# A new plan of a batch, and maxima taken from three PSUM banks at once, in a kernel of cross attention and experts

## The chip, the cores and the metric

The kernel runs on one core of a Trainium2 chip. The metric is the device time of one execution in microseconds (us); three runs of a kernel give a median. The engines of a core are TensorE (PE in the profile, its weight loads PEld), VectorE (DVE), ScalarE (ACT), GpSimd (POOL) and SyncE (SP), which here issues the DMA transfers. PSUM, into which TensorE writes, has 8 banks of 512 float32 columns.

## The reference, cut to what matters

```
x = x + tanh(g_xattn) * xattn(layernorm(x), ctx)     # x: 16 x 100 x 128, ctx: 16 x 1444 x 96, 16 heads of 64
x = x + tanh(g_ffn)   * ffn(layernorm(x))

xattn: q = x w_q; k = ctx w_k; v = ctx w_v           # per head
       softmax(q k^T / 8) v, then w_o and b_o
ffn:   rmsnorm, self attention over 100 tokens (16 heads of 8), wo, residual,
       rmsnorm, router (softmax, top 2 of 8 experts), experts of width 256 and one shared
```

The softmax of the cross attention is computed with a maximum subtracted for each row of `q`, the 1600 rows of a batch being 16 heads times 100 tokens.

## The kernel before, in words

The 16 batches run one after the other. The weights are folded in advance, so that a batch needs `qk = x M` (1600 rows of 96 numbers) and scores `qk ctx^T` against the 1444 context rows. All large products are in float16 with a second float16 part for the remainder (`_hi`, `_lo`), so a product takes three matmuls.

**Units.** A batch has 24 units `i` (two halves of the rows times 12 chunks of 128 context rows). In unit `i` TensorE computes the scores of chunk `i` (`score_unit`, L736 to L738, six matmuls), ScalarE takes their exponential twice (`probs`: `p32` in float32, `p_hi` in float16), VectorE or GpSimd the remainder `p_lo` (L430; GpSimd in the units of `LO_POOL`), and TensorE multiplies the probabilities of unit `i - 2` by the context (`pv_unit`, L755: `p_hi` with `c_hi`, `p_hi` with `c_lo`, `p_lo` with `c_hi`). Scores use banks 0 to 2, two for a unit, so the second half of the scores of unit `i` waits until ScalarE is through with unit `i - 1`. Banks 3 and 4 hold the sums.

**The ring of three.** All other small work of a batch is cut into numbered pieces, which a table `plan` places in the units: `q` (the rows `qk` of the next batch), `p` (maxima), `m` (the transpose of the maxima), `y0` and `y1` (the output projection of one half), `f0` to `f16` (the self attention of the batch before), `ln`, `rs`, `xf`, `h2` (norms). The pieces of a unit are divided into thirds: some stand behind the scores, some behind the first third of the value matmuls (`middle`), some behind the last. The same list is walked by TensorE, ScalarE and VectorE. Each piece with a matmul takes the next of the banks 5 to 7 in turn, and TensorE waits only until the piece three places back has been read:

```
ring, bank = (2, 1 + k % 2) if kind in ("prep", "end") else (3, (base[0] + k) % 3)
last = order[k - ring] if k >= ring else None
```

**The maxima.** The rows of the next batch form 13 tiles (`RT`) of 128, and the 1444 columns three parts (`MP`) of 512, 512 and 420. Piece `p` n is one matmul into one bank (L835) and one VectorE reduction to `mx` (L1281); after the last, VectorE reduces `mx` to `mx_row` and negates it to `mneg`. `m` transposes `mneg` (L839), VectorE copies it to `mrow` (L1291), and SP sends it as an extra row into `qk_hi` (`send_row`), where the first scores of the next batch wait for it (`row_in`). Ahead of the first batch a form `w` does the same with the other banks, two sets of three in turn: three matmuls (L815) and one reduction over 1444 columns (L1256).

**The context.** `ctx_hi_parts` (ScalarE) and `ctx_lo` (GpSimd) convert the context of batch `b + 1` at the start of batch `b`; SP then has it transposed into `cT_both` (L491), for which the first `p` of the batch waits (`ct_in`), and copied to `c_both`. One planner's rule places the `p`: each goes to the unit of 4 to 20 with the least `load`, a sum of estimated costs.

GpSimd also normalises the sums of a half (`normalise`) and does `norm_1` and `norm_2` for the self attention. The first batch and the last have lists of their own; the experts follow the last batch.

Of the kernel before, what the change touches and what calls it, by code (L numbers as in the profile page):

```python
# [29 lines left out]
def flamingo_kernel(nc, x, ctx, g_xattn, g_ffn, w_q, w_k, w_v, w_o, b_o, norm1_w, norm2_w,  # L30
# [35 lines left out]
    for n, i in enumerate((0, 0, 1, 1)):  # L66
        plan[i].append(("q", n))
    plan[7].append(("y1", 0))
    plan[20].append(("y0", 0))
    plan[7].append(("ln", 0))  # L70
    plan[7].append(("xf", 0))
    for n, i in enumerate((9, 10, 11, 12, 13, 14, 13, 14, 15, 16, 15, 16, 17, 18, 19, 20, 23)):
        plan[i].append(("f", n))
# [58 lines left out]
    PREPARE = ("y0", "q", "p", "m")  # L132
# [42 lines left out]
    def batch_of(unit, b):  # L175

        return b + {"q": 1, "p": 1, "m": 1, "y0": 0}.get(unit[0], -1)
# [10 lines left out]
                "pad qk_hi0", "pad qk_hi1", "lnr0", "minus one", "pad p_hi", "pad p_lo", "mx", "ones v9", "ones mask",  # L188
# [13 lines left out]
    with ExitStack() as stack:  # L202
# [36 lines left out]
        mx = sb("mx", [P, RT, MP])  # L239
# [100 lines left out]
        def run_aux(aux, units, b, kind, parity):  # L340
# [5 lines left out]
            order = [u for u in at if u[0] not in NO_BANK]  # L346
            for u in units:
# [194 lines left out]
        def _(pool):  # L542
# [31 lines left out]
            step("mx", g.memset(mx[:, :, :], 0.0))  # L574
# [111 lines left out]
        def _(pe):  # L686
# [101 lines left out]
            def aux(seq, free, par, unit, b, parity, out_of, last):  # L788
# [15 lines left out]
                if kind == "w":  # L804
                    if n == 0:
                        pe.wait_ge(ct_in, 16)
                    if n == 1:
# [3 lines left out]
                    if n >= 2:  # L811
# [572 lines left out]
```

## Time and profile before

| | before |
|---|---|
| median of 3 runs | 1397.75 us (1396.24 to 1400.17) |
| the profiled execution, its own time | 1400.51 us |
| its span | 1398.8 us |
| mean granted TensorE clock | 0.982 |
| busy: PE, DVE, ACT, POOL | 90%, 74%, 58%, 47% |
| DMA | 57.27 MB, 41 GB/s on the mean |

The busy share is the union of an engine's instructions over the span. The span goes from the first to the last instruction; what lies around it (1400.51 against 1398.8) isn't in the trace. The granted clock is 1.00 at 2.4 GHz and 0.50 at 1.2 GHz.

### The profile page before, as it was taken

How to read it: one execution, taken by the hardware profiler on the slowest of the kernel's cores; microseconds unless marked ns; L12 is line 12 of the kernel's file. 1: busy time of each engine (PE TensorE's matmuls, PEld its weight loads, DVE VectorE, ACT ScalarE, POOL GpSimd, SP SyncE). 2: the span in 40 equal slices, each digit the busy share in tenths (PEclk: the TensorE clock that was granted, in tenths of full speed). 3: DMA queues.
4: the chain of work that ended last, by engine and by line, in shares of the span. 5: the costliest groups of instructions: out<-in, count | busy, mean ns of one | idle time of the engine just before them, and what ended most of it. 6: DMA issues, size and time to landing. Idle time of an engine off the chain costs nothing.

```text
span 1398.8 us, 34572 instructions
## 1 busy us (share of the span) xinstructions
PE 1265.0 (90%) x14472; PEld 912.5 (65%) x14472; DVE 1034.4 (74%) x1762; ACT 818.2 (58%) x1476; POOL 661.4 (47%) x555
## 2 busy tenths in 40 slices
PE   6789798989999999999998989899999999889998
PEld 4366576766666666667675767676666666557776
DVE  5797777768686868596868687786868685866776
ACT  1346466665666565666565656656665666555664
POOL 3135355454544554444444545445354454544654
PEclk9799999999999999999999999999999999999999
DMA  6204303030313030302112030303031200010000
GB/s 162 62 2 111 78 13 76 13 75 13 76 12 76 12 76 12 71 11 50 35 32 56 13 76 13 76 13 76 13 76 13 60 13 15 1 26 2 8 8 13
DMA packets 122277, 57.27 MB, mean 41 GB/s; under 512 B 108262, under 2 KB 117706, under 8 KB 122122
## 3 DMA queue, kind: packets, MB, share of 16 engines
q1 hardware_dynamic: 122122, 55.07, 17.5%
q8 instruction: 114, 1.87, 0.6%
q14 instruction: 41, 0.34, 0.1%
HBM read 15.38 MB, written 0.82 MB: 12 GB/s over the span
## 4 chain that ended last, share of the span: by engine, by line
PE 59%; DVE 20%; ACT 11%; DMA 5%; issue 4%; POOL 0%; SPq 0%; ACTq 0%; DVEq 0%; POOLq 0%
PE psum L755 13%; DVE p_lo L430 9%; PE psum L736 7%; PE psum L835 7%; PE psum L737 6%; PE psum L738 6%; DMA cT_both<-c_new 5%; PE psum L771 4%; DVE mx L1281 3%; PE psum L867 3%; ACT p_hi L964 3%; PE psum L783 3%; ACT p_hi L959 2%; ACT p L963 2%; PE psum L889 2%
## 5 line engine op out<-in xcount | busy, mean ns | idle before, releaser
L430 POOL TENSOR_TENSOR p_lo<-p,p_hi 128x768 f16<-128x768 f32 (+1 forms) x144 | 273.7, 1905 | 412.8 <-ACT p_hi L959 261.5
L1281 DVE TENSOR_REDUCE mx<-psum 128x1 f32<-128x512 f32 (+1 forms) x585 | 355.0, 651 | 70.6 <-PE psum L835 66.6
L958 ACT ACTIVATE p<-psum 128x768 f32<-128x768 f32 (+1 forms) x256 | 214.0, 836 | 276.7 <-PE psum L738 276.7
L430 DVE TENSOR_TENSOR p_lo<-p,p_hi 128x768 f16<-128x768 f32 (+1 forms) x240 | 326.3, 1359 | 28.6 <-ACT p_hi L959 25.5
L755 PEld LDWEIGHTS psum<-c_both,p_hi 128*128 128x128 f16 x4992 | 283.1, 99 | 88.9 <-issue 31.6
L755 PE MATMUL psum<-c_both,p_hi 128*128 128x97 f16 (+1 forms) x4992 | 326.1, 207 | 5.5 <-ACT acc_sb L974 5.4
L736 PE MATMUL psum<-qk_hi,cT_both 97*128 97x384 f16 (+1 forms) x768 | 259.7, 338 | 30.1 <-ACT p_hi L959 19.4
L737 PE MATMUL psum<-qk_lo,cT_both 96*128 96x384 f16 (+1 forms) x768 | 258.5, 337 | 0.0
L738 PE MATMUL psum<-qk_hi,cT_both 96*128 96x384 f16 (+1 forms) x768 | 256.3, 334 | 0.0
L835 PE MATMUL psum<-cT_both,qk_hi 96*128 96x512 f16 (+1 forms) x585 | 201.9, 371 | 30.7 <-DVE mx L1281 14.3
L963 ACT ACTIVATE p<-psum 128x384 f32<-128x384 f32 (+1 forms) x256 | 130.0, 508 | 151.0 <-PE psum L738 151.0
L959 ACT ACTIVATE p_hi<-psum 128x768 f16<-128x768 f32 (+1 forms) x256 | 213.4, 834 | 0.0
L755 PE MATMUL psum<-c_both,p_lo 128*128 128x97 f16 x2496 | 172.8, 208 | 20.1 <-POOL p_lo L430 16.9
L755 PEld LDWEIGHTS psum<-c_both,p_lo 128*128 128x128 f16 x2496 | 129.9, 99 | 23.1 <-POOL p_lo L430 19.2
L736 PEld LDWEIGHTS psum<-qk_hi,cT_both 97*128 97x128 f16 x768 | 75.6, 98 | 97.5 <-ACT p_hi L959 49.5
L964 ACT ACTIVATE p_hi<-psum 128x384 f16<-128x384 f32 (+1 forms) x256 | 131.0, 512 | 0.0
L738 PEld LDWEIGHTS psum<-qk_hi,cT_both 96*128 96x128 f16 x768 | 76.1, 99 | 57.9 <-issue 2.2
L737 PEld LDWEIGHTS psum<-qk_lo,cT_both 96*128 96x128 f16 x768 | 76.1, 99 | 45.8 <-issue 1.4
L645 POOL TENSOR_TENSOR p_lo<-p,p_hi 128x400 f16<-128x400 f32 x72 | 69.2, 962 | 67.9 <-ACT p_hi L986 67.9
L835 PEld LDWEIGHTS psum<-cT_both,qk_hi 96*128 96x128 f16 x585 | 54.0, 98 | 58.8 <-DVE mx L1281 21.5
L594 POOL TENSOR_TENSOR acc_rc<-acc_sb,minus_one 128x6 f32<-128x6 f32 (+1 forms) x31 | 52.9, 1706 | 50.3 <-ACT acc_sb L974 50.3
L1227 DVE TENSOR_TENSOR qk_lo<-psum,qk_hi 96x400 f16<-96x400 f32 x64 | 34.0, 566 | 49.8 <-ACT qk_hi L935 49.7
(201 smaller groups left out, 2082.2 us busy)
## 6 DMA issues: line engine op xcount, KB each, us to landing
c_both<-c_new SPq DMA_DIRECT2D x16, 768.0 KB, 4.0
ctx_nat<-in_ctx_dram SPq DMA_DIRECT2D x16, 528.0 KB
aT<-a_new SPq DMA_TRANSPOSE x64, 2.9
wg<-in_L_ffn_e_gate_dram SPq DMA_DIRECT2D x1, 1024.0 KB, 5.5
wu<-in_L_ffn_e_up_dram SPq DMA_DIRECT2D x1, 1024.0 KB, 7.9
wd<-in_L_ffn_e_down_dram SPq DMA_DIRECT2D x8, 128.0 KB, 5.1
out_dram<-x SPq DMA_DIRECT2D x4, 200.0 KB
x<-in_x_dram SPq DMA_DIRECT2D x1, 600.0 KB
```

The costliest lines, as they stand in the source:

```text
L430: engine.tensor_tensor(p_lo[0:m, i % 3, 0:w], p32[0:m, i % 3, 0:w], p_hi[0:m, i % 3, 0:w], ALU.subtract).then_inc(lo_made(b, i)[0], 1)
L645: g.tensor_tensor(hid_lo[:, n % HS, :], hidden[:, n % 3, :], hid_hi[:, n % HS, :], ALU.subtract).then_inc(hid_lo_out, 1)
L736: mm(outs[k], cT_hi[parity][:, cols], qk_hi[parity][:, qs[k]], start=True, stop=False)
L737: mm(outs[k], cT_hi[parity][0:C, cols], qk_lo[parity][:, qs[k]], start=False, stop=False)
L738: t = mm(outs[k], cT_lo[parity][:, cols], qk_hi[parity][0:C, qs[k]], start=False, stop=True)
L755: t = mm(psum[:, ACCB + bank, k * (C + 1):k * (C + 1) + wide], p[0:m, i % 3, n * P:(n + 1) * P], c[parity][0:m, j, 0:wide], start=(j == 0 ...
L835: t = mm(bank[:, 0:w], qk_hi[parity][0:C, padded_rows(rt)], cT_hi[parity][0:C, part * MW:part * MW + w], start=True, stop=True)
L958: a(to32, src, ACT.Exp, scale=DH ** -0.5)
L959: ins = a(to_hi, src, ACT.Exp, scale=DH ** -0.5)
L963: a(to32[:, k, :], src, ACT.Exp, scale=DH ** -0.5)
L964: ins = a(to_hi[:, k, :], src, ACT.Exp, scale=DH ** -0.5)
L1281: v.tensor_reduce(mx[:, rt, part:part + 1], bank[:, 0:w], AX.X, ALU.max)\
```

## The change

A planner's rule for 39 single-bank pieces `p` is replaced by 13 pieces `w`, one for each row tile, placed first in the 13 units of 3 to 21 that a sum of costs finds lightest. `w`, which only the start of the kernel used, now also works inside the batches: TensorE waits until all three ring banks are read, fills banks 5, 6 and 7, VectorE reads all three with one reduction straight to `mx_row`, and the next ring piece waits for that reduction (`wide`). `mx` and its final reduction go. The other entries of the plan move too: one `q` in each of units 0 to 3 in place of two in 0 and two in 1; `y1`, `ln`, `xf` and `norm_1` from unit 7 to 6, `f0` and `f1` to 8 and 9, `m` from 21 to 22, GpSimd's remainders from (5, 7, 9, 11, 13, ...) to (4, 5, 8, 10, 12, ...). The context of batch `b + 2` is converted in units 18 (ScalarE) and 19 (GpSimd) of batch `b`, not that of `b + 1` at its start.

```
-    for n, i in enumerate((0, 0, 1, 1)):
+    for n, i in enumerate((0, 1, 2, 3)):
         plan[i].append(("q", n))
...
-    CTX_AT, NORM1_AT, ACC0_AT, NORM2_AT = 0, 7, 14, 22
-    LO_POOL = (5, 7, 9, 11, 13, 16, 18, 20, 22)
+    CTX_HI_AT, CTX_LO_AT, NORM1_AT, ACC0_AT, NORM2_AT = 18, 19, 6, 14, 22
+    LO_POOL = (4, 5, 8, 10, 12, 16, 18, 20, 22)
...
-    plan[21].append(("m", 0))
+    places = range(3, 22)
+    for n, i in enumerate(sorted(sorted(places, key=lambda i: (load[i], i))[0:RT])):
+        plan[i].insert(0, ("w", n))
+    plan[22].append(("m", 0))
...
+                before = ringed[:ringed.index(u)] if u in ringed else []
+                wide = (b + 1) * RT + sum(o[0] == "w" for o in before) if before and before[-1][0] == "w" else 0
...
+        def wide_bank(b, n):
+            return AUXB if b else 3 * (n % 2)
...
                 for i in range(UNITS):
+                    if i == CTX_LO_AT and b + 2 < B:
+                        ctx_lo(b + 2, parity)
...
+                    if b:
+                        pe.wait_ge(aux_free, free)
+                        pe.wait_ge(*last)
+                        pe.wait_ge(wide_free, b * RT + n)
                     for part in range(MP):
                         cols = slice(part * MW, min(KV, (part + 1) * MW))
-                        t = mm(psum[:, 3 * (n % 2) + part, 0:cols.stop - cols.start], qk_hi[parity][0:C, padded_rows(n)],
-                               cT_hi[parity][0:C, cols], start=True, stop=True)
+                        t = mm(psum[:, wide_bank(b, n) + part, 0:cols.stop - cols.start],
+                               qk_hi[parity][0:C, padded_rows(n)], cT_hi[parity][0:C, cols], start=True, stop=True)
                     t.then_inc(wide_full, 1)
                 if kind in NO_BANK:
                     return
                 if seq >= 2:
                     pe.wait_ge(*last)
+                if wide:
+                    pe.wait_ge(wide_free, wide)
...
-                elif kind == "p":
-                    rt, part = divmod(n, MP)
-                    if n == 0:
-                        pe.wait_ge(aux_free, free)
-                        pe.wait_ge(ct_in, (b + 1) * 16)
-                    w = min(MW, KV - part * MW)
-                    t = mm(bank[:, 0:w], qk_hi[parity][0:C, padded_rows(rt)],
-                           cT_hi[parity][0:C, part * MW:part * MW + w], start=True, stop=True)
...
                 for i in range(UNITS):
-                    if i == CTX_AT and kind != "last":
-                        ctx_hi_parts(b + 1, kind, 1 - parity)
+                    if kind == "first" and i == 0:
+                        ctx_hi_parts(1, kind, 1)
+                    if i == CTX_HI_AT and b + 2 < B:
+                        ctx_hi_parts(b + 2, kind, parity)
...
                 if kind == "w":
-                    dve.wait_ge(wide_full, n + 1)
-                    scores_of = psum[:, 3 * (n % 2):3 * (n % 2) + MP, :].rearrange("p b w -> p (b w)")[:, 0:KV]
+                    dve.wait_ge(wide_full, b * RT + n + 1)
+                    scores_of = psum[:, wide_bank(b, n):wide_bank(b, n) + MP, :].rearrange("p b w -> p (b w)")[:, 0:KV]
                     v.tensor_reduce(mx_row[:, n:n + 1], scores_of, AX.X, ALU.max).then_inc(wide_free, 1)
```

In a middle batch `w0` to `w12` stand in units 4, 5, 6, 7, 8, 10, 11, 13, 15, 16, 17, 19 and 21. In 4, 5, 7 and 10 `w` stands alone and so last; in 8 (`w4`, `f0`), 11 (`w6`, `f2`), 17 (`w10`, `f12`), 19 (`w11`, `f14`) and 21 (`w12`, `rs`) it stands in the middle; in 6 (`w2`, `y1`), 13 (`w7`, `f4`, `f6`), 15 (`w8`, `f8`, `f10`) and 16 (`w9`, `f9`, `f11`) it stands first.

The first place is TensorE's stream in unit 13 of a middle batch, from the last score on (`f6` is L885 before, L883 after). Before, `f4` (L880) is the first piece there, and a `p` (L835) the last:

```order
L738 MATMUL psum<-qk_hi,cT_both 128x416
L880 MATMUL psum<-kbd,qT 100x400 [waits aux_free]
L755 MATMUL psum<-c_both,p_hi 128x97 x6
L885 MATMUL psum<-ident,ex 100x100 [waits exp_out,aux_free]
L885 MATMUL psum<-ident,ex 100x100 x3
L755 MATMUL psum<-c_both,p_hi 128x96 x6
L755 MATMUL psum<-c_both,p_lo 128x97 [waits lo_pool]
L755 MATMUL psum<-c_both,p_lo 128x97 x5
L835 MATMUL psum<-cT_both,qk_hi 128x512 [waits aux_free]
```

After (`f4` is L878):

```order
L738 MATMUL psum<-qk_hi,cT_both 128x416
L819 MATMUL psum<-cT_both,qk_hi 128x512 [waits wide_free,aux_free]
L819 MATMUL psum<-cT_both,qk_hi 128x512
L819 MATMUL psum<-cT_both,qk_hi 128x420
L755 MATMUL psum<-c_both,p_hi 128x97 x6
L878 MATMUL psum<-kbd,qT 100x400 [waits wide_free,aux_free]
L755 MATMUL psum<-c_both,p_hi 128x96 x6
L755 MATMUL psum<-c_both,p_lo 128x97 [waits probs_lo]
L755 MATMUL psum<-c_both,p_lo 128x97 x5
L883 MATMUL psum<-ident,ex 100x100 [waits exp_out,aux_free]
```

The three matmuls of a tile stand together at the start of the unit, and `f4` has moved behind them with a wait for their reader; six value matmuls lie between.

The second place is VectorE's stream from the copy for `f0` to the maxima of `f2` (L1306 before, L1296 after), with `kbd`, the block-diagonal keys of `f1`, between. Before:

```order
L1297 COPY hT<-psum 128x100 [waits aux_full]
L430 TENSOR_TENSOR p_lo<-p,p_hi 128x768 [waits pv,probs_hi]
L1281 TENSOR_REDUCE mx<-psum 128x1 [waits aux_full] x2
L1299 COPY qT<-psum 128x100 [waits aux_full]
L1300 COPY v<-psum 100x16x8
L1301 TENSOR_TENSOR kbd<-psum,head_mask 128x1600
L1281 TENSOR_REDUCE mx<-psum 128x1 [waits aux_full]
L430 TENSOR_TENSOR p_lo<-p,p_hi 128x768 [waits pv,probs_hi]
L1306 TENSOR_REDUCE mx<-psum 100x4 [waits aux_full]
```

After:

```order
L1287 COPY hT<-psum 128x100 [waits aux_full]
L1289 COPY qT<-psum 128x100 [waits aux_full]
L1290 COPY v<-psum 100x16x8
L1291 TENSOR_TENSOR kbd<-psum,head_mask 128x1600
L430 TENSOR_TENSOR p_lo<-p,p_hi 128x768 [waits pv,probs_hi]
L1256 TENSOR_REDUCE mx_row<-psum 128x1 [waits wide_full] x2
L1296 TENSOR_REDUCE mx<-psum 100x4 [waits aux_full]
```

Two wide reductions (`w5`, `w6`), with a remainder and `kbd` ahead of them, stand in front of the maxima of `f2` in place of three narrow ones.

The third place is TensorE's stream at the end of a batch, from the value matmuls of unit 22 to the first score of the next batch. Before, the transpose of the maxima (L839) stands in front of unit 22; after (below), it is L837 and stands behind it:

```order
L755 MATMUL psum<-c_both,p_lo 128x97 x6
L837 MATMUL psum<-ident,mneg 13x128 [waits max_step,wide_free,aux_free]
L736 MATMUL psum<-qk_hi,cT_both 128x416 [waits probs_hi]
L737 MATMUL psum<-qk_lo,cT_both 128x416
L738 MATMUL psum<-qk_hi,cT_both 128x416
L736 MATMUL psum<-qk_hi,cT_both 128x416 [waits probs_hi]
L737 MATMUL psum<-qk_lo,cT_both 128x416
L738 MATMUL psum<-qk_hi,cT_both 128x416
```

One unit lies between the transpose and the first score that needs the row, where two lay before.

## Rows read from the trace of the kernel before

**Rows 1.** The page, busy time, share of the span and instructions of each engine

```profile
PE 1265.0 (90%) x14472; PEld 912.5 (65%) x14472; DVE 1034.4 (74%) x1762; ACT 818.2 (58%) x1476; POOL 661.4 (47%) x555
```

**Rows 2.** One middle batch: busy PE, PEld, DVE, ACT, POOL, clock, DMA

```profile
584.00:658.00 74.00, 68.62 (x829) 49.79 (x827) 55.23 (x91) 46.16 (x84) 35.95 (x28) 1.00 0.21 42
```

**Rows 3.** The chain that ended last: start, us, what

```profile
155.71 1.51 PE psum L867 x27
...
606.07 3.90 DVE p_lo L430
...
1191.74 1.52 PE psum L867 x27
```

**Rows 4.** Timeline of TensorE in one batch, its longest waits, in brackets

```profile
586.68 0.68 PE L755 MATMUL psum<-c_both,p_hi 128*128 128x97 f16 x12 [0.38 <-ACT acc_sb L974]
...
590.31 0.34 PE L736 MATMUL psum<-qk_hi,cT_both 97*128 97x384 f16 x1 [0.38 <-ACT p_hi L959]
...
592.05 0.38 PE L835 MATMUL psum<-cT_both,qk_hi 96*128 96x512 f16 x1 [1.08 <-DMA cT_both<-c_new]
...
607.61 0.43 PE L755 MATMUL psum<-c_both,p_lo 128*128 128x97 f16 x6 [1.02 <-POOL p_lo L430]
...
613.41 0.89 PE L880 MATMUL psum<-kbd,qT 128*100 128x400 f32 x2 [1.19 <-DVE kbd L1301]
...
650.86 0.35 PE L736 MATMUL psum<-qk_hi,cT_both 97*128 97x416 f16 x1 [0.40 <-ACT p_hi L964]
```

**Rows 5.** Timeline of TensorE, unit 5 of that batch and the next score

```profile
593.44 0.33 PE L736 MATMUL psum<-qk_hi,cT_both 97*128 97x384 f16 x1
...
594.42 0.38 PE L835 MATMUL psum<-cT_both,qk_hi 96*128 96x512 f16 x1
594.64 0.42 PE L755 MATMUL psum<-c_both,p_hi 128*128 128x97 f16 x6
...
595.64 0.34 PE L835 MATMUL psum<-cT_both,qk_hi 96*128 96x420 f16 x1
595.82 0.33 PE L736 MATMUL psum<-qk_hi,cT_both 97*128 97x384 f16 x1
```

**Rows 6.** Timeline of VectorE in that batch, narrow reductions

```profile
592.46 0.69 DVE L1281 TENSOR_REDUCE mx<-psum 128x1 f32<-128x512 f32 x1 [3.53 <-PE psum L835]
...
596.50 3.48 DVE L1281 TENSOR_REDUCE mx<-psum 128x1 f32<-128x512 f32 x6
```

**Rows 7.** Wide reductions ahead of batch 0: timelines, then the group by form

```profile
26.50 4.80 DVE L1256 TENSOR_REDUCE mx_row<-psum 128x1 f32<-128x1444 f32 x3 [0.65 <-PE psum L815]
...
37.19 11.09 DVE L1256 TENSOR_REDUCE mx_row<-psum 128x1 f32<-128x1444 f32 x7
...
28.22 1.38 PE L815 MATMUL psum<-cT_both,qk_hi 96*128 96x512 f16 x3 [0.56 <-DVE mx_row L1256]
...
L1256 DVE TENSOR_REDUCE mx_row<-psum 128x1 f32<-128x1444 f32 x13 | 20.7, 1655 | 0.8 <-PE psum L815 0.6
```

**Rows 8.** Timelines: the row of maxima, a middle batch, then the first

```profile
573.86 0.22 PE L839 MATMUL psum<-ident,mneg 128*13 128x128 f16 x1
...
578.83 0.33 PE L736 MATMUL psum<-qk_hi,cT_both 97*128 97x384 f16 x1
...
49.01 0.21 DVE L1291 COPY mrow<-psum 13x128 f16<-13x128 f16 x1 [0.45 <-PE psum L839]
...
51.91 0.50 PE L736 MATMUL psum<-qk_hi,cT_both 97*128 97x384 f16 x1 [2.94 <-DMA qk_hi<-mrow]
```

**Rows 9.** Timeline of TensorE in batch 0; stretches as in rows 2

```profile
74.30 0.93 PE L843 MATMUL psum<-ident,x 100*128 100x100 f32 x4 [1.66 <-DVE mx L1281]
...
72.00:75.00 3.00, 1.34 (x12) 1.13 (x11) 2.90 (x5) 0.00 (x0) 0.00 (x0) 0.50 0.00 0
75.00:78.00 3.00, 3.00 (x16) 1.66 (x15) 2.93 (x7) 0.81 (x2) 0.00 (x0) 0.50 0.00 0
...
611.00:614.00 3.00, 1.81 (x14) 1.09 (x13) 3.00 (x6) 1.51 (x2) 0.41 (x1) 1.00 0.00 0
```

More of the change, by code:

```diff
@@ L65, in flamingo_kernel @@
     plan = {i: [] for i in range(UNITS)}
-    for n, i in enumerate((0, 0, 1, 1)):
+    for n, i in enumerate((0, 1, 2, 3)):
         plan[i].append(("q", n))
-    plan[7].append(("y1", 0))
+    plan[6].append(("y1", 0))
     plan[20].append(("y0", 0))
-    plan[7].append(("ln", 0))
-    plan[7].append(("xf", 0))
-    for n, i in enumerate((9, 10, 11, 12, 13, 14, 13, 14, 15, 16, 15, 16, 17, 18, 19, 20, 23)):
+    plan[6].append(("ln", 0))
+    plan[6].append(("xf", 0))
+    for n, i in enumerate((8, 9, 11, 12, 13, 14, 13, 14, 15, 16, 15, 16, 17, 18, 19, 20, 23)):
         plan[i].append(("f", n))
@@ L175, in batch_of @@
     def batch_of(unit, b):
-        return b + {"q": 1, "p": 1, "m": 1, "y0": 0}.get(unit[0], -1)
+        return b + {"q": 1, "w": 1, "m": 1, "y0": 0}.get(unit[0], -1)
     F_STEPS = ["stats", "aggr", "qT", "v", "mx0", "mx1", "mx2", "mx3", "rc0", "rc1", "rc2", "rc3",
@@ L187, in flamingo_kernel @@
     SET_POOL = ["-1/2", "zero ident", "ident", "zero ident16", "ident16", "zero c_new", "ones c_new", "ones end",
-                "pad qk_hi0", "pad qk_hi1", "lnr0", "minus one", "pad p_hi", "pad p_lo", "mx", "ones v9", "ones mask",
+                "pad qk_hi0", "pad qk_hi1", "lnr0", "minus one", "pad p_hi", "pad p_lo", "ones v9", "ones mask",
                 "mask above", "head_mask", "zero a_new", "n1"] + [f"rank of {e}" for e in range(E)] + \
@@ L238, in flamingo_kernel @@
         aT = sb("aT", [P, 2, sum(TILES) * P], F16)
-        mx = sb("mx", [P, RT, MP])
         mx_row = sb("mx_row", [P, RT])
@@ L346, in run_aux @@
             order = [u for u in at if u[0] not in NO_BANK]
+            ringed = [u for u in at if u[0] == "w" or u[0] not in NO_BANK]
             for u in units:
@@ L354, in run_aux @@
                 last_free = at[last][1] + 1 if last else 0 if kind == "end" else k - ring + 1
+                if u[0] == "w":
+                    last = next((o for o in reversed(order[:k]) if by_act(o)), None)
+                before = ringed[:ringed.index(u)] if u in ringed else []
+                wide = (b + 1) * RT + sum(o[0] == "w" for o in before) if before and before[-1][0] == "w" else 0
                 aux(base[0] + k, base[1] + free, bank, u, on, (parity + near) % 2,
@@ L357, in run_aux @@
                     (pt_out, batch_of(last, b) * 4 + (last[1] - 5)) if last and by_act(last)
-                    else (aux_free, base[1] + last_free))
+                    else (aux_free, base[1] + last_free), wide if kind not in ("prep", "end") else 0)
         def cut(q, n):
@@ L648, in body @@
             def body(b, kind, parity):
-                if kind != "last":
-                    ctx_lo(b + 1, 1 - parity)
                 if kind == "first":
+                    ctx_lo(1, 1)
                     token_rstd(1)
@@ L786, in down, with aux @@
                 t.then_inc(down_full, 1)
-            def aux(seq, free, par, unit, b, parity, out_of, last):
+            def aux(seq, free, par, unit, b, parity, out_of, last, wide):
                 kind, n = unit
@@ L805, in aux @@
                     if n == 0:
-                        pe.wait_ge(ct_in, 16)
-                    if n == 1:
+                        pe.wait_ge(ct_in, (b + 1) * 16)
+                    if n == 1 and not b:
                         set_wait(pe, set_act, SET_ACT, "wvT")
@@ L1000, in router_exp_step, with aux @@
                     a(t, t, ACT.Exp).then_inc(router_exp, 1)
-            def aux(seq, free, par, unit, b, parity, out_of, last):
+            def aux(seq, free, par, unit, b, parity, out_of, last, wide):
                 if unit[0] == "q":
@@ L1206, in result, with aux @@
                 stt(x2[:, four, :], x2[:, four, :], tf[0:S, 0:1], x1[:, four, :], ALU.mult, ALU.add).then_inc(fin, 1)
-            def aux(seq, free, par, unit, b, parity, out_of, last):
+            def aux(seq, free, par, unit, b, parity, out_of, last, wide):
                 kind, n = unit
@@ L1277, in aux @@
                     return
-                if kind == "p":
-                    rt, part = divmod(n, MP)
-                    w = min(MW, KV - part * MW)
-                    v.tensor_reduce(mx[:, rt, part:part + 1], bank[:, 0:w], AX.X, ALU.max)\
-                        .then_inc(aux_free, 1)
-                    if n == NPU - 1:
-                        dve.wait_ge(aux_free, free + 1)
-                        v.tensor_reduce(mx_row[:, :], mx[:, :, :], AX.X, ALU.max).then_inc(max_step, 1)
-                        dve.wait_ge(max_step, b * 2 + 1)
-                        ts(mneg[:, :], mx_row[:, :], -1.0, SHIFT, ALU.mult, ALU.add).then_inc(max_step, 1)
-                elif kind == "m":
+                if kind == "m":
                     if not (isinstance(b, int) and b == 0):
```

18 lines of the change are left out of this document (3 added, 15 removed).

## Prediction, made before the changed kernel ran

> **What bounds the kernel now.** I read the page first: TensorE is busy for 90% of the span and VectorE for 74% [rows 1]. Then the stretches: one middle batch, 584 to 658 us, has 68.62 us of busy TensorE in 74, at a granted clock of 1.00, which is the 2.4 GHz level [rows 2]. So TensorE's own stream bounds a batch, with about 5.4 us of recorded idle in it. The chain that ended last gives the batch's length: the 27 matmuls of `y1` start at 155.71 in batch 1 and at 1191.74 in batch 15, so 14 batches take 1036.0 us, 74.0 each [rows 3].
>
> The timeline of TensorE shows where the idle lies. The six longest waits of a batch [rows 4] are for ScalarE (0.38, 0.38 and 0.40: the next exponential or the evacuation of the sums), for the transposed context from the DMA (1.08), for a remainder on GpSimd (1.02) and for `kbd` on VectorE (1.19). A matmul's recorded duration outlasts the start of its successor by some 0.16 us, so each such wait costs TensorE about 0.16 us more than the row says. With the small gaps that have no entry I count 7.7 us of waits in the batch that starts at 578.83 and takes 73.6 us. That leaves 65.9 us of TensorE work per batch, which the change keeps.
>
> **The unit in pieces.** In [rows 5] unit 5 runs from 593.44 to 595.82. Its scores take 0.98 (1.06 from unit 12 on), the three `p` pieces 0.22, 0.22 and 0.18 = 0.62, and the three thirds of the value matmuls the rest, 0.78, so 0.26 each (0.31 with seven tiles).
>
> **What the change adds: an exchange over three banks.** Before, a `p` takes one bank, and TensorE waits only for the reader three ring units back. After, a `w` waits until all three banks are read, fills them, and the next ring unit waits for the end of its one VectorE instruction. The time from the start of `w` on TensorE to the release of its follower has rows for each part. The third matmul starts after 0.42 and lasts 0.34; VectorE starts within 0.03 of a matmul's recorded end (592.05 + 0.38 against 592.46) [rows 4, 6]; the reduction takes 1.655 [rows 7]; TensorE starts 0.07 after it (26.50 + 1.655 against 28.22) [rows 7]. Sum: 0.79 + 1.66 + 0.07 = 2.52 us. TensorE's cover is 0.60 (its own three matmuls) and what stands between `w` and its follower:
>
> First, `w` at the start of a unit and its follower in the middle (units 6, 13, 15, 16): cover 0.60 + 0.26 or 0.31, wait 1.6 to 1.66; four times, 6.6 us. Second, `w` in the middle and its follower at the end (8, 11, 17, 19): cover 0.60 + 0.52 or 0.61, wait 1.3 to 1.4, in unit 8 1.46 with `p_lo` ahead of it on VectorE; four times, 5.5 us. Third, `w` at the end of a unit and the next `w` in the next unit: nearly hidden from 4 to 5 (0.14), 0.92 from 5 to 6, 0.66 from 7 to 8, and 0.97 from 10 to 11, where VectorE still has `kbd` and a `p_lo`; 2.7 us. Fourth, `w` waits for a reader that the ring of three let slip before: `kbd` before `w5` 0.69, the maxima of `f3` 0.33, the copy of `f7` 0.30; 1.3 us.
>
> Together 16.05 us per batch. Behind the waiting matmul stand, in TensorE's order, value matmuls and the next scores, so ScalarE and VectorE starve a moment later. A bound from below for an exchange is nothing (VectorE late anyway, TensorE waiting at its next semaphore instead), and from above the full 1.72 of [rows 7] at all 13, 22 us.
>
> **What VectorE saves.** Six reductions in a row take 3.48 us for 2888 columns, seven wide ones 11.09 for 10108 [rows 6, 7]. At 1.04 ns a column that is about 0.06 us of fixed time for each instruction, thus 26 x 0.06 = 1.6 us a batch, and 0.2 for the final reduction. VectorE is not the bound, so I credit nothing. The Trainium skill, page "Perfetto Trace Analysis", section "Optimizing Scalar/DVE Operations", says that grouping helps when the engine is saturated, and that breaking instructions up helps when it is not but causes bubbles elsewhere. By that rule this change goes the wrong way, as in the count above. The Trainium skill gives there an overhead of some 125 ns for a VectorE access to PSUM, which would make the saving 3.3 us a batch, an estimate from that page, where the rows in sequence give 1.6.
>
> **The other moves.** The context of batch b+1 is converted in units 18 and 19 of batch b-1, not at the start of b; SP's order is the same, but it now finds the conversion done and issues the transposition right behind the row of maxima. That removes 1.08 + 0.16. ScalarE and GpSimd are 58% and 47% busy, and take the conversion beside TensorE's waits: 0. `norm_1` and GpSimd's remainders stand a unit earlier: the wait of 1.02 goes. The wait of 1.19 for `kbd` goes into the exchanges. One `q` in each of units 0 to 3 fills units 2 and 3, which had no other work; I leave 0.36 at unit 0, 0.5 for the evacuation in unit 2, 0.22 in unit 14, 0.37 in unit 23: 1.45 us. The transpose `m` stands one unit later: its row of maxima had 4.97 us (573.86 to 578.83), and from the copy's start to the first score that uses it the transfer took 2.90 (49.01 to 51.91) [rows 8]. Now only unit 23, some 2.5 us, lies between; with 0.3 from transpose to copy the row comes 0.7 us late. Bounds: 0 and 1.5.
>
> So a batch becomes 65.9 + 16.05 + 1.45 + 0.7 = 84.1 us, 10.1 more than 74.0.
>
> **The clock.** The stream will have waits of 0.92 and 1.66 us with 0.86 of work between them in unit 6. The trace has one such place: after the wait of 1.66 at 74.30 the granted clock was 0.50, the 1.2 GHz level, for 72 to 78 us, while a stretch with 1.81 of 3 us busy, 611 to 614, kept 1.00 [rows 9]. In those 6 us TensorE was busy for 4.34, half of which, 2.2, is what the low level cost. I count one such drop a batch, 31 us in all; bounds 0, and four drops (units 6, 8, 11, 13), 123.
>
> **The sum.** The first batch has five exchanges with a follower in the same unit, 5 x 1.5 = 8 us, and its long wait for the context gets 2 us more cover. Against the profiled execution's own time: 1400.5 + 14 x 10.1 (141) + 8 - 2 + 31 = 1579. The median of the runs is 2.8 below that execution, so 1576.
>
> **The rivals.** The forecast (0.50): exchanges as counted, up to one drop of the clock in most batches, 1540 to 1610.
>
> The clock falls often (0.17). The row at 74.30 speaks for it; against it stands the middle batch with three waits over 1 us and a clock of 1.00 [rows 2, 4]. Four drops a batch: 1545 + 123 = 1668. The Trainium skill, page "TensorE: Matmul & The Clock Gate", section "A second HAM failure mode: psum-queue depth-cycling", tells of short idles from cycling through PSUM banks that made the clock oscillate. By that rule this case is the likely one; the rows at 611 to 614 do not bear it out.
>
> Half of it hides (0.21). From 606 on the chain runs over VectorE for a while, 3.90 us in one `p_lo` [rows 3], so waits there would only change their name. With 8 of the 16 us real: 14 x 2 + 8 = 36, 1434, and up to 1540 with more.
>
> Faster (0.06): the exchanges fall on moments when TensorE waits for the next exponential anyway, and the removed waits remain as gain: (1.08 + 1.02 + 1.19 + 3 x 0.16) + 1.0 from units 2 and 3 = 4.8 us a batch, 1398 - 67 = 1331. It decides where an exchange costs under 4.8 / 13 = 0.37 us; I count 1.23. Against it speaks the order: behind each follower stand matmuls that ScalarE fed long before.
>
> No change that can be measured (0.02): within 0.3%, about what a measurement of this kernel can tell from none. The chances of the cases of this list and of what lies beyond them (0.04, slower) give slower 0.92.
>
> The range of 1480 to 1675 takes in the forecast, most of the case of the clock and the upper part of the half-hidden one.
>
> **What would show it.** In the changed profile the idle of TensorE before `y1`, `f0`, `f2`, `f4`, `f8`, `f9`, `f12`, `f14` would be put down to the wide reduction at L1256, 1.1 to 1.5 us each as recorded; the idle before the wide matmuls at L819 to L1256, `kbd` or a copy; the period of `y1` would be near 84 to 86 us; VectorE's busy share would fall to some 60%. The wait for the context in unit 4 would be gone, and one for the row of maxima would stand at unit 0. A period under 78 us, or a wide reduction that starts late because VectorE is busy with `p_lo`, would make me wrong; so would drops of the clock in every exchange.

## The result, and the profile after

The changed kernel takes 1681.74 us, the median of 4 runs (1662.92 to 1685.47), against 1398.96 for the kernel before (1396.24 to 1400.68) on the same chip. The ratio is 1.200, 95% interval 1.190 to 1.209: slower, as forecast, but by 283 us and not by 177. The time lies above the range. The profiled execution took 1678.04 us, with a span of 1676.3, beside 1398.8 before.

The page, busy time of each engine over the span, answers to [rows 1]:

```profile
PE 1382.5 (82%) x14472; PEld 976.8 (58%) x14472; DVE 972.1 (58%) x1357; ACT 823.2 (49%) x1476; POOL 662.8 (40%) x554
```

TensorE ran the same 14472 matmuls, but was busy for 117 us more. At an unchanged count busy time grows a little with every break in the stream, since a recorded duration outlasts the start of its successor; growth of this size points at slower matmuls, and the mean granted clock is 0.92, beside 0.98 before. VectorE shows 62 us less work and a share that fell from 74% to 58%: it has become idler, and the kernel slower.

The chain that ended last, as in [rows 3] (start, us, what):

```profile
168.79 3.09 PE psum L865 x27
...
1474.67 1.52 PE psum L865 x27
```

The 27 matmuls of `y1` start 14 batches apart at 168.79 and 1474.67, so a batch takes 93.3 us, where 84.1 and 2.2 for the clock were forecast. The first of them took 3.09 us where [rows 3] has 1.51; the granted clock over these 3.09 us is 0.50.

The timeline of TensorE around the batch from 822.29, its waits in brackets and rows without a wait left out, and one row of VectorE, answers to [rows 4] and shows the exchange:

```profile
819.73 0.77 PE L819 MATMUL psum<-cT_both,qk_hi 96*128 96x512 f16 x3 [0.86 <-DVE mx_row L1256]
...
820.53 1.66 DVE L1256 TENSOR_REDUCE mx_row<-psum 128x1 f32<-128x1444 f32 x1 [0.95 <-PE psum L819]
...
822.29 0.23 PE L865 MATMUL psum<-Nh_hi,aT 96*100 96x128 f16 x1 [1.54 <-issue]
...
828.71 0.77 PE L819 MATMUL psum<-cT_both,qk_hi 96*128 96x512 f16 x3 [0.58 <-DVE mx_row L1256]
831.28 0.28 PE L869 MATMUL psum<-ident,hn 100*128 100x100 f32 x1 [1.28 <-issue]
836.32 0.78 PE L819 MATMUL psum<-cT_both,qk_hi 96*128 96x512 f16 x3 [0.52 <-DVE kbd L1291]
838.94 0.77 PE L819 MATMUL psum<-cT_both,qk_hi 96*128 96x512 f16 x3 [0.60 <-DVE mx_row L1256]
841.51 0.89 PE L878 MATMUL psum<-kbd,qT 128*100 128x400 f32 x2 [1.28 <-issue]
...
848.91 0.89 PE L878 MATMUL psum<-kbd,qT 128*100 128x400 f32 x2 [1.58 <-DVE mx_row L1256]
852.65 0.48 PE L755 MATMUL psum<-c_both,p_hi 128*128 128x97 f16 x7 [0.92 <-ACT acc_sb L972]
...
856.12 0.77 PE L819 MATMUL psum<-cT_both,qk_hi 96*128 96x512 f16 x3 [0.26 <-issue]
858.69 0.52 PE L883 MATMUL psum<-ident,ex 100*100 100x100 f32 x4 [1.49 <-issue]
863.98 0.52 PE L883 MATMUL psum<-ident,ex 100*100 100x100 f32 x4 [1.50 <-issue]
869.57 0.84 PE L887 MATMUL psum<-v,pT 100*100 100x9 f32 x8 [1.20 <-issue]
880.12 0.28 PE L891 MATMUL psum<-ident,sctx 100*128 100x100 f32 x1 [1.20 <-issue]
...
892.06 0.32 PE L736 MATMUL psum<-qk_hi,cT_both 97*128 97x384 f16 x1 [0.55 <-DMA qk_hi<-mrow]
```

From the start of `w` at 819.73 to its follower at 822.29 it is 2.56 us, and 2.57 from 828.71 to 831.28 and from 838.94 to 841.51. VectorE starts 0.80 after `w` and takes 1.66. The trace puts several of these waits down to "issue", which names no releaser. The times do: 820.53 + 1.66 = 822.19, and the follower starts 0.10 later. Eight followers wait in this way, for 1.20 to 1.58 us, and five `w` for 0.26 to 0.86. The context's wait of 1.08 in [rows 4] is gone, and one for the row of maxima, 0.55, stands at unit 0.

Stretches of the changed kernel, columns as in rows 2. First two whole batches, then parts of them:

```profile
724.05:822.29 98.24, 82.28 (x815) 57.31 (x816) 51.37 (x63) 46.08 (x82) 36.12 (x28) 0.86 0.15 32
822.29:911.71 89.42, 72.82 (x816) 51.70 (x816) 51.78 (x63) 46.08 (x82) 36.11 (x28) 0.96 0.15 35
724.05:728.00 3.95, 3.95 (x41) 3.68 (x42) 1.19 (x4) 0.00 (x0) 0.36 (x1) 0.57 0.02 4
734.00:740.00 6.00, 5.34 (x40) 3.92 (x41) 1.74 (x5) 1.51 (x2) 0.52 (x1) 0.72 0.01 3
764.00:770.00 6.00, 5.17 (x41) 3.20 (x39) 2.20 (x4) 2.25 (x5) 0.67 (x1) 0.72 0.17 33
772.00:776.00 4.00, 4.00 (x26) 2.18 (x26) 0.40 (x3) 1.77 (x3) 0.00 (x0) 0.57 0.01 4
778.00:795.00 17.00, 16.34 (x128) 11.97 (x128) 5.21 (x10) 4.98 (x8) 5.98 (x4) 0.60 0.01 1
870.00:878.00 8.00, 8.00 (x56) 5.74 (x56) 1.68 (x5) 3.01 (x6) 4.22 (x3) 0.58 0.01 2
```

Both batches issue the same program, yet one takes 98.24 and the other 89.42. The second has a single low stretch, 870 to 878; between 724 and 795 the first has five. Over all 14 batches, in windows of 1 us, it is the same picture: none is without a low stretch, six have a single one that amounts to 6 to 7 us at the low level, and the other eight have three to six, 17 to 27 us together. Busy time times what the clock lacks gives the cost: 3.95 x 0.43 + 5.34 x 0.28 + 5.17 x 0.28 + 4.00 x 0.43 + 16.34 x 0.40 = 12.9 us, against 8.00 x 0.42 = 3.4. The difference, 9.5, is that of the two PE busy times, 82.28 and 72.82, and about that of their lengths, 8.8.

### The profile page after: what moved, and what is told of

Read it like the earlier page. It is cut to its first block, busy times and chain, and to the rows that moved or that the text cites. A ratio compares the mean times of both kernels' runs of the same rounds, so it can differ in the third digit from the quotient of the medians.

```text
span 1676.3 us, 34421 instructions
## 1 busy us (share of the span) xinstructions
PE 1382.5 (82%) x14472; PEld 976.8 (58%) x14472; DVE 972.1 (58%) x1357; ACT 823.2 (49%) x1476; POOL 662.8 (40%) x554
## 4 chain that ended last, share of the span: by engine, by line
PE 61%; DVE 16%; issue 12%; ACT 7%; DMA 2%; SPq 0%; POOL 0%; ACTq 0%; DVEq 0%; POOLq 0%
PE psum L755 15%; PE psum L819 8%; DVE mx_row L1256 7%; PE psum L736 6%; PE psum L738 6%; PE psum L737 6%; PE psum L771 4%; PE psum L865 3%; PE psum L887 3%; PE psum L783 2%; PE psum L878 2%; DVE p_lo L430 2%; DVE kbd L1291 2%; DMA qk_hi<-mrow 2%; ACT p_hi L962 2%
## 5 line engine op out<-in xcount | busy, mean ns | idle before, releaser
L1256 DVE TENSOR_REDUCE mx_row<-psum 128x1 f32<-128x1444 f32 x208 | 344.7, 1661 | 249.0 <-PE psum L819 247.5
L430 POOL TENSOR_TENSOR p_lo<-p,p_hi 128x768 f16<-128x768 f32 (+1 forms) x144 | 251.0, 1747 | 564.2 <-ACT p_hi L957 259.6
L755 PEld LDWEIGHTS psum<-c_both,p_hi 128*128 128x128 f16 x4992 | 297.1, 103 | 130.4 <-issue 52.0
L736 PE MATMUL psum<-qk_hi,cT_both 97*128 97x384 f16 (+1 forms) x768 | 274.3, 357 | 25.3 <-DMA qk_hi<-mrow 13.3
L430 DVE TENSOR_TENSOR p_lo<-p,p_hi 128x768 f16<-128x768 f32 (+1 forms) x240 | 283.6, 1182 | 7.1 <-ACT p_hi L957 4.2
L737 PE MATMUL psum<-qk_lo,cT_both 96*128 96x384 f16 (+1 forms) x768 | 276.4, 360 | 0.0
L738 PE MATMUL psum<-qk_hi,cT_both 96*128 96x384 f16 (+1 forms) x768 | 274.9, 358 | 0.0
L819 PE MATMUL psum<-cT_both,qk_hi 96*128 96x512 f16 (+1 forms) x624 | 183.0, 407 | 57.7 <-DVE mx_row L1256 36.0
L755 PE MATMUL psum<-c_both,p_lo 128*128 128x97 f16 x2496 | 181.4, 214 | 3.6 <-DVE p_lo L430 1.9
L978 ACT ACTIVATE ex<-ex 100x400 f32<-100x400 f32 x64 | 34.4, 537 | 120.2 <-DVE ex L1297 120.1
```

The lines of the kernel that those rows point to most:

```text
L430: engine.tensor_tensor(p_lo[0:m, i % 3, 0:w], p32[0:m, i % 3, 0:w], p_hi[0:m, i % 3, 0:w], ALU.subtract).then_inc(lo_made(b, i)[0], 1)
L736: mm(outs[k], cT_hi[parity][:, cols], qk_hi[parity][:, qs[k]], start=True, stop=False)
L737: mm(outs[k], cT_hi[parity][0:C, cols], qk_lo[parity][:, qs[k]], start=False, stop=False)
L738: t = mm(outs[k], cT_lo[parity][:, cols], qk_hi[parity][0:C, qs[k]], start=False, stop=True)
L755: t = mm(psum[:, ACCB + bank, k * (C + 1):k * (C + 1) + wide], p[0:m, i % 3, n * P:(n + 1) * P], c[parity][0:m, j, 0:wide], start=(j == 0 ...
L819: t = mm(psum[:, wide_bank(b, n) + part, 0:cols.stop - cols.start], qk_hi[parity][0:C, padded_rows(n)], cT_hi[parity][0:C, cols], start=Tr ...
```

## The experiments

**Is it the clock? Work added to the waits.**

```diff
                     t.then_inc(wide_full, 1)
+                    for _ in range({2: 24, 7: 24, 8: 24, 9: 24, 4: 20, 6: 20, 10: 20, 11: 20}.get(n, 0) if b else 0):
+                        mm(psum[:, ACCB + 1, 4 * (C + 1):512], qk_hi[parity][0:C, padded_rows(n)],
+                           cT_hi[parity][0:C, 0:512 - 4 * (C + 1)], start=False, stop=False, skip_group_check=True)
```

> The changed kernel with work added: behind the w of units 6, 13, 15, 16 stand 24, and behind that of units 8, 11, 17, 19 20 more matmuls of 124 columns into unused columns of an accumulator bank, about 1.2 and 1.0 us, inside the wait for the wide reduction. Nothing reads them. Theory (clock drops beyond one a batch make up the difference to the forecast): the exchange waits keep their length, TensorE works through most of them, the clock stays near 1.00, and the kernel with more work is faster: 1570 to 1630 us, period 86 to 89. Rival (the waits themselves are longer than counted and the clock follows from them without costing much): 1670 to 1710 us. Second rival (the fillers fill more than the wait and delay the work): above 1710.

Measured: 1582.3 us (1581.66 to 1582.62), ratio to before 1.129 (1.127 to 1.132). 2640 more matmuls made the changed kernel 99 us faster. One batch of this kernel, stretch columns as above:

```profile
862.25:948.47 86.22, 79.08 (x991) 59.08 (x992) 50.74 (x63) 46.06 (x82) 36.87 (x28) 1.00 0.16 36
```

Its timeline of TensorE around unit 6, with the added matmuls at L823:

```profile
859.68 0.77 PE L819 MATMUL psum<-cT_both,qk_hi 96*128 96x512 f16 x3 [0.86 <-DVE mx_row L1259]
860.28 1.46 PE L823 MATMUL psum<-cT_both,qk_hi 96*128 96x124 f16 x24
...
862.25 0.23 PE L868 MATMUL psum<-Nh_hi,aT 96*100 96x128 f16 x1 [0.24 <-issue]
```

Two rows of its chain, 14 batches apart:

```profile
170.14 1.68 PE psum L868 x27
...
1378.11 1.52 PE psum L868 x27
```

The exchange is as long as ever (859.68 to 862.25, 2.57), but only 0.24 of the wait is idle. The granted clock is 1.00, and the period (1378.11 - 170.14) / 14 = 86.3. So the clock costs 93.3 - 86.3 = 7.0 us a batch, and the waits cost what they cost whether TensorE idles or not.

**Is it the exchange or the other moves?** First the three-bank form replaced by the one-bank form, once by the planner's load and once in threes at the places of `w`; then the reverse, the exchange with the other moves undone (only `m` stays in unit 22).

```diff
 (moves alone: the changed plan, with one-bank pieces)
-    for n, i in enumerate(sorted(sorted(places, key=lambda i: (load[i], i))[0:RT])):
-        plan[i].insert(0, ("w", n))
+    for n in range(NPU):
+        i = min(share, key=lambda i: (load[i], i))
...
+            plan[i].append(("p", n))
 (three together)
+        plan[i][0:0] = [("p", n * MP + k) for k in range(MP)]
 (exchange alone: the plan of before, with)
+    for n, i in enumerate((4, 5, 6, 7, 8, 10, 11, 13, 15, 16, 17, 19, 21)):
+        plan[i].insert(0, ("w", n))
+    plan[22].append(("m", 0))
```

> The kernel before with every move of the change but the exchange: q, y1, ln, xf, norm_1, f0, f1, the GpSimd list, m in unit 22 and the context conversion as in the changed kernel, and 39 single-bank p pieces spread over the units by the planner's load. Theory by the terms of the prediction: waits of 1.08, 1.02 and 0.5 go, the row of maxima costs 0.7: 1345 to 1385 us, period 71 to 73. Rival (the row of maxima or the context of the sums late, as with three p together, 1432 us): 1395 to 1430.

> All other moves of the change are kept (one q in each of units 0 to 3, y1, ln, xf and norm_1 a unit earlier, the new GpSimd list, the context conversion in units 18 and 19, m in unit 22), and at each of the 13 places of w stand three single-bank p pieces with three narrow reductions. Theory (the exchange over three banks costs the time): a p waits only for the reader three ring pieces back, so the 16 us of exchange waits and the clock drops go and the gains of the other moves remain: 1360 to 1410 us, period of y1 72.5 to 74.5, granted clock 1.00. Rival (the new order of the units costs it, whatever the form of the maxima): above 1550 us. In between, 1420 to 1550, both have a share.

> The three-bank w with its wide reduction stands in the same 13 units, m stays in unit 22, and every other move of the change is undone (q in units 0, 0, 1, 1, y1 and norm_1 in unit 7, f0 and f1 in 9 and 10, the old GpSimd list, the context conversion at the start of the batch). Theory: about as slow as the changed kernel, 1640 to 1720 us, clock 0.90 to 0.94, the wait for the context back in unit 4. Rival (order of the units): below 1480 us.

Measured: moves alone 1341.6 us, ratio 0.959 (0.955 to 0.962); three together 1432.1, ratio 1.022 (1.018 to 1.026); exchange alone 1661.8, ratio 1.187 (1.183 to 1.190). The exchange alone came as the theory had it, and it is slower by 262 us, though the wait for the context, expected back in unit 4, isn't in the timeline of the batch shown next. The moves alone are a gain of 57, a little more than their theory had (1345 to 1385 us, a period of 71 to 73). One batch of the exchange alone, stretch columns as above:

```profile
632.03:721.44 89.41, 69.75 (x815) 49.55 (x816) 53.82 (x64) 46.09 (x82) 36.21 (x28) 1.00 0.16 35
```

Its clock stayed at 1.00, with eight followers of `w` waiting for 1.20 to 1.58 us, and it still takes 89.4 us. So here the exchanges, with `m` a unit later, cost 89.4 - 74.0 = 15.4 us a batch with no lower clock in it and no matmul added. Its neighbour, 721.44 to 816.61, takes 95.2.

One batch of the moves alone:

```profile
719.12:789.15 70.03, 67.71 (x818) 49.38 (x817) 52.15 (x91) 46.25 (x82) 38.71 (x28) 1.00 0.21 44
```

The only waits that its timeline of TensorE lists between 740 and 810 are these:

```profile
766.95 0.35 PE L737 MATMUL psum<-qk_hi,cT_both 97*128 97x416 f16 x1 [0.27 <-ACT p_hi L960]
771.73 0.32 PE L737 MATMUL psum<-qk_hi,cT_both 97*128 97x384 f16 x1 [0.52 <-DMA qk_hi<-mrow]
778.19 0.68 PE L756 MATMUL psum<-c_both,p_hi 128*128 128x97 f16 x12 [0.45 <-ACT acc_sb L975]
```

The three together missed their range: 1432.1 us and 76.4 a batch, not 1360 to 1410 and 72.5 to 74.5. That is between the theory and its rival, where both have a share. The longest waits in the timeline of one batch, and two rows of VectorE ahead of the second:

```profile
793.37 0.48 PE L749 MATMUL psum<-c_both,p_hi 128*128 128x97 f16 x7 [1.44 <-ACT acc_sb L968]
...
797.44 1.95 DVE L423 TENSOR_TENSOR p_lo<-p,p_hi 128x832 f16<-128x832 f32 x1
...
799.32 1.18 DVE L1277 TENSOR_REDUCE mx<-psum 128x1 f32<-128x512 f32 x2
800.05 0.87 PE L883 MATMUL psum<-v,pT 100*100 100x9 f32 x8 [1.60 <-DVE mx L1277]
804.53 0.87 PE L883 MATMUL psum<-v,pT 100*100 100x9 f32 x8 [0.66 <-DVE mx L1277]
```

The piece at 800.05 starts while the last of three narrow reductions still runs, so the one it waits for is the second, the first of the two at 799.32. VectorE came to it only behind a remainder of 1.95 us. With three together, a ring piece thus waits for a reduction of its own unit and for whatever VectorE does ahead of it. So of the 340 us between moves alone and the changed kernel, bunching alone explains about 90.

**How the cost goes with the length of the reading.** The changed kernel, with the reduction cut to fewer columns, so that the maxima are incomplete.

```diff
-                    scores_of = psum[...].rearrange("p b w -> p (b w)")[:, 0:KV]
+                    scores_of = psum[...].rearrange("p b w -> p (b w)")[:, 0:256]
 (and in the other kernel)
+                    scores_of = psum[...].rearrange("p b w -> p (b w)")[:, 0:KV // 2]
```

> The changed kernel with one thing less: the wide reduction reads 256 of the 1444 columns, so the maxima are incomplete. The reduction takes some 0.33 us in place of 1.66, the exchange 1.2 in place of 2.5. Theory (the length of the exchange beyond TensorE's cover is the cost, and the clock drops follow from it): 16 us of waits a batch shrink to about 3, the drops go: period of y1 74 to 77, 1390 to 1450 us, clock 1.00. Rival (it is the giving up of the ring, all three banks at once, whatever the reading takes; the scores behind it starve): above 1520 us, clock still under 0.97.

> The changed kernel, whose wide reduction reads 722 of the 1444 columns, so the maxima are incomplete: 0.81 us, exchange 1.67. Between the kernel with 256 columns (period 73.0, clock 1.00) and the changed one (93.3). Account by cover: first to middle 4 x 0.8, middle to end 4 x 0.5, so about 5 us more than with 256 columns, period 77 to 79 with the clock at 1.00: 1420 to 1465 us. Rival (waits of some 0.8 us already pull the clock down): above 1490.

Measured: 256 columns 1377.5 us, ratio 0.983 (0.981 to 0.985); 722 columns 1440.0, ratio 1.028 (1.024 to 1.032). The group of the reduction (busy, mean ns | idle before) in the first:

```profile
L1256 DVE TENSOR_REDUCE mx_row<-psum 128x1 f32<-128x256 f32 x208 | 88.1, 424 | 239.8 <-PE psum L819 239.5
```

In the second:

```profile
L1256 DVE TENSOR_REDUCE mx_row<-psum 128x1 f32<-128x722 f32 x208 | 188.9, 909 | 210.6 <-PE psum L819 208.7
```

In the changed kernel:

```profile
L1256 DVE TENSOR_REDUCE mx_row<-psum 128x1 f32<-128x1444 f32 x208 | 344.7, 1661 | 249.0 <-PE psum L819 247.5
```

The periods are 73.1, 77.2 and, with the clock kept up by the added matmuls, 86.3, for readings of 0.42, 0.91 and 1.66 us. From the first to the second a batch grows by 4.1 us for 0.49 more in each reduction, that is as if 8 or 9 of the 13 exchanges were bare; from the second to the third by 9.1 for 0.75, as if 12 were. That is TensorE's cover being used up, as in the forecast's count. Both short readings keep a mean clock of 0.99. Even with 256 columns a batch takes 3.1 us more than in the moves alone (73.1 against 70.0; 36 us in all), so giving up three banks at once has a small price of its own, some of it the part of the shorter exchange that TensorE still doesn't cover.

**More cover: `w` last in its unit.**

```diff
-        plan[i].insert(0, ("w", n))
+        plan[i].append(("w", n))
```

> The changed kernel with w as the last ring piece of its unit in place of the first (same 13 units), so that the next unit's scores, 0.98, stand between it and its follower. Account by cover: exchange waits fall from 12.1 to some 4 us a batch, but w now waits for the reader of the f piece just ahead of it, 8 times about 0.5: together 8 in place of 16, few or no clock drops, period 77 to 81, 1440 to 1530 us. Rival (the waits only change place, since three free banks are needed at once wherever w stands): above 1600.

Measured: 1486.6 us, ratio 1.062 (1.058 to 1.066), period 79.8, clock 0.98: in the range of the account. Two rows of its timeline of TensorE show both sides of it, a wait shortened to 0.56 behind the next scores, and a `w` that now waits for the reader of the piece ahead:

```profile
731.44 0.28 PE L869 MATMUL psum<-ident,hn 100*128 100x100 f32 x1 [0.56 <-issue]
...
742.98 0.77 PE L819 MATMUL psum<-cT_both,qk_hi 96*128 96x512 f16 x3 [0.81 <-DVE ex L1297]
```

One word in the plan is worth 195 us. It is still 145 us behind the moves alone.

**Where the clock's drops start.** The added matmuls in unit 6 only.

```diff
+                    for _ in range({2: 24}.get(n, 0) if b else 0):
```

> The changed kernel with 24 more matmuls only behind the w of unit 6. In the changed kernel's trace batches of 89 and of 97 us follow each other: the longer ones have y1 and unit 8 at a clock of 0.5, and four or five low stretches, the shorter ones a single one around unit 16. Theory (each drop follows the waits just ahead of it, and those of unit 6 set off the first of a long batch): y1 takes 1.7 us in every batch and the low stretches of the first 15 us go, 1610 to 1660 us. Rival (the low stretches come anyway, at other places): 1670 to 1690.

Measured: 1660.0 us, but with 1651.05 to 1685.61 in four runs; ratio 1.185 (1.179 to 1.191). The changed kernel's own runs start at 1662.92, so the gain in time is hardly clear of their spread. The profiled execution was the slowest of the four, 20 us above the next, and its lengths are not typical of the others. In it the `y1` of all the middle batches takes 1.68 us, so the low clock is gone from unit 6, yet the batches still take 89 to 96 us, with a low stretch later in the batch (859 to 884 in the one from 820.72). Half of the expectation held, and the time does not separate it from its rival well. Why long and short batches follow each other stays open.

**Which of the moves gain.** The context conversion moved alone; with `y1`, `ln`, `xf`, `norm_1`, `f0`, `f1` and the GpSimd list; with the four `q`; and all moves with `m` back in unit 21.

```diff
 (all three: context conversion in units 18 and 19 as in the change)
 (the second)
-    LO_POOL = (5, 7, 9, 11, 13, 16, 18, 20, 22)
+    LO_POOL = (4, 5, 8, 10, 12, 16, 18, 20, 22)
...
+    plan[6].append(("y1", 0))
 (the third)
-    for n, i in enumerate((0, 0, 1, 1)):
+    for n, i in enumerate((0, 1, 2, 3)):
 (the fourth, against all moves)
-    plan[22].append(("m", 0))
+    plan[21].append(("m", 0))
```

> The kernel before with one move: the conversion of the context in units 18 and 19 of the batch before, not at the start. The wait of 1.08 + 0.16 for the transposed context goes: 14 x 1.24 = 17 us less, 1375 to 1390. Rival (the wait only changes its name, as ScalarE or the row of maxima end the next one): 1393 to 1405.

> The kernel before with the early context conversion and with y1, ln, xf, norm_1, f0, f1 and the GpSimd list a unit earlier; q and m as before. The context alone gave 1403. If GpSimd's remainder (a wait of 1.02 + 0.16) and kbd (1.19 + 0.16) are the rest of what the moves gain, the period falls from 74.4 to about 72: 1360 to 1375 us. Rival (the gain comes with one q in each of units 0 to 3): 1390 to 1405.

> The kernel before with the early context conversion and one q in each of units 0 to 3, all else as before. By the terms, 1.0 us a batch for units 2 and 3: period 73.4, 1383 to 1393 us. Rival (the two pieces of q in one unit are what holds up the batch's start, and with them gone the waits of 0.62 and 1.10 for the narrow reductions go too): 1355 to 1375.

> The kernel with all moves but the exchange (1342 us, period 70.0), with the transpose m back in unit 21. There the row of maxima shows a wait of 0.52 at unit 0. Term of the prediction (m a unit later makes the row late): the wait goes, period 69.4 to 69.9, 1332 to 1341 us. Rival (m so soon behind the last reductions waits for them itself, or the wait changes its name to ScalarE): 1342 to 1352.

Measured: context alone 1403.1 us, ratio 1.003 (1.001 to 1.005); with the GpSimd list and `norm_1` 1340.4, 0.959 (0.956 to 0.962); with `q` 1402.9, 1.003 (1.001 to 1.004); all moves with `m` in 21 1333.7, 0.954 (0.952 to 0.956). The context alone missed, and came as its rival had it: the wait of 1.08 is gone from its timeline, but two for narrow reductions stand in the units around it, with the old wait for GpSimd behind them.

```profile
744.72 0.39 PE L836 MATMUL psum<-cT_both,qk_hi 96*128 96x512 f16 x1 [0.62 <-DVE mx L1284]
748.36 0.39 PE L836 MATMUL psum<-cT_both,qk_hi 96*128 96x512 f16 x1 [1.10 <-DVE mx L1284]
...
758.73 0.43 PE L756 MATMUL psum<-c_both,p_lo 128*128 128x97 f16 x6 [1.02 <-POOL p_lo L430]
```

The wait had covered a late VectorE. With the remainder of unit 4 on GpSimd and the `norm_1` group a unit earlier, all of these go, and 63 us with them, more than the two waits that I had summed (14 x 2.4 = 34). Of this group I moved everything at once, so which part of it does it is argued and not shown. The context with `q` missed both its ranges, 1383 to 1393 and the rival's 1355 to 1375. One `q` in each of units 0 to 3 is worth nothing while those waits stand (1403.1 and 1402.9), and 7 us once they are gone: between 1340.4 and 1333.7 the four `q` are the only difference. `m` in unit 21 takes the wait for the row of maxima away and is worth 8 us (1341.6 and 1333.7). All moves with `m` in 21 is the fastest kernel that ran.

## Why the prediction was right in sign and short in size

Per batch, in us, against its own steps:

| term | forecast | measured | from |
|---|---|---|---|
| batch without exchanges | 65.9 + 1.45 + 0.7 = 68.05 | 70.0 | moves alone |
| exchanges | 16.05 | 16.3 | 86.3 with added matmuls - 70.0 |
| clock | 2.2 | 7.0 | 93.3 - 86.3 |
| sum | 86.3 | 93.3 | |

That the forecast's sum and the kernel with added matmuls both have 86.3 is chance: the one has 2.2 for the clock in it, the other 2.0 more for the rest of the batch.

**The step that failed is the clock.** "I count one such drop a batch, 31 us in all." The price of one was low, 2.2 us against 3.4 in the short batch. Above all the number was wrong: six of the fourteen batches have one, the others three to six. 14 x (7.0 - 2.2) = 67 of the missing 106 us. The rival "the clock falls often", 1668 us at 0.17, is the case that came. I had set it aside because one stretch of [rows 9], 611 to 614, kept 1.00 with 1.81 of 3 us busy, and the middle batch had three waits over 1 us [rows 4]. Those waits stand alone, with microseconds of full work on both sides; here they come in eight units of a batch. A single row of a healthy stream says nothing of such a sequence.

The row that spoke for the rival was also misread. The prediction has the clock at 0.50 after the wait of 1.66 at 74.30. The rows ahead of it in batch 0 are these:

```profile
69.36 0.39 PE L835 MATMUL psum<-cT_both,qk_hi 96*128 96x512 f16 x1 [0.83 <-DVE mx L1281]
70.83 0.85 PE L835 MATMUL psum<-cT_both,qk_hi 96*128 96x512 f16 x2 [0.82 <-DVE mx L1281]
...
69.00:72.00 3.00, 1.71 (x16) 1.08 (x17) 2.96 (x6) 1.07 (x2) 0.73 (x1) 0.93 0.00 0
```

In windows of 1 us the clock is 1.00 up to 71, 0.78 from 71 to 72 and 0.50 from 72 on. So it had begun to fall before the wait of 1.66 began (74.30 - 1.66 = 72.64), behind waits of 0.74, 1.07, 0.83 and 0.82 (61.58 to 70.83). The trace of before thus already had a drop behind a sequence of waits, none of them as long as the 1.20 to 1.58 of the followers here.

The measured runs speak for the rule weighed in the rival: granted 0.96 and 0.86 in two batches of the same program, and 1.00 once the waits are filled. The waits don't settle it alone, since a batch of the exchange alone kept 1.00 with them; what sets off a drop in one batch and not in its neighbour is not shown. The Trainium skill, page "TensorE: Matmul & The Clock Gate", section "A second HAM failure mode: psum-queue depth-cycling", tells of a kernel whose micro-idles from cycling through PSUM banks make the clock swing between its two levels. By that rule, the trace agrees.

**The exchanges** were right in mechanism and size: 2.56 to 2.57 us where 2.52 was worked out from rows of the kernel before, 16.3 a batch against 16.05. Added up from the rows of the batch shown, with 0.16 for each wait, the eight followers cost 12.35 (12.1 forecast) and the five `w` 3.6 (4.0), 16.0 together. Single waits lie close too: 0.86 against 0.92 before `w` in unit 6, 0.52 against 0.69 behind `kbd`. The half-hidden rival did not come; nor the faster one, though its other half is real, since the removed waits are worth 4.0 a batch (74.0 - 70.0).

**The rest of the batch** was 2.0 us short, 28 us in all. The three waits listed for the moves alone are 1.24, with 0.16 each 1.7, of the 70.0 - 65.9 = 4.1; the remainder lies in gaps that have no entry, and I have not placed it. Gaps of that size were there before: the seven waits with an entry in the batch of [rows 4] (the six shown and one of 0.21) come to 4.66, with 0.16 each 5.8, of the 7.7 counted. The forecast took the other 1.9 for idle that goes, and as much is still there. The row of maxima was rightly sized: waits of 0.52 to 0.55 at unit 0. Unit 14's wait for the sums was 0.92, not 0.22; the moves alone have no such wait, so it lies in the 16.3.

**The ends**: the first `y1` starts at 168.79 and not at 155.71, 13.1 later, and what follows the last is 201.6 and not 207.1; together 7.6 against 6 forecast. The profiled execution of after lies 3.7 below its median, that of before 2.8 above, which is the last 6.5 of the 106.

**VectorE's saving** is there, 62 us, and worth nothing, as credited. It is 3.5 to 3.9 us a batch (55.23 against 51.78 and 51.37), twice the 1.6 + 0.2 counted: the six reductions in a row leave 3.48 - 3.00 = 0.48 us beside their columns, 0.08 each and not 0.06, and the rest is not placed. The Trainium skill, page "Perfetto Trace Analysis", section "Optimizing Scalar/DVE Operations", says that where such an engine is not saturated but makes others idle, breaking its instructions up may let work finish sooner; by that rule, the runs agree, 1342 us with 39 narrow reductions spread over the units and 1682 with 13 wide.

## What to carry to other kernels

Before giving a ring's banks to one large reading, set the length of the whole exchange (fill, read, release) against what the other engine has to do between the fill and its next need for a bank. What sticks out is paid in full, every time, however idle the reader is. Then ask what the waits do to TensorE's clock: a stream that lost a microsecond or more in eight of its 24 units (16.3 us a batch) here lost nearly half as much again (7.0) to the lower level, and that cost jumps about between equal batches. A removed wait is a gain only if the engine named next is not late as well; the context's move gave nothing until GpSimd's share was shifted too.

## What was not expected of the hardware

2640 added matmuls with no use took 99 us off, while the granted clock rose from 0.92 to 0.98 over the span. The long reductions fit 1.04 ns a column plus 0.16 us (424, 909 and 1661 ns for 256, 722 and 1444 columns, each by itself); the six in a row leave 0.08 each. And batches of one loop body took from 89.1 to 98.2 us within one execution.
